# Attention scores in two 64-row tiles of the array, with the exponential banks and the maximum banks paired, and another slot order

## The reference, cut to what matters

```
def mha(x, mask, Wi, bi, Wo, bo):          # encoder: 16 heads of 8 features, causal, ALiBi bias
    q, k, v = split(x @ Wi.T + bi)
    scores = q @ k.T / sqrt(8) + mask      # per head, 256 x 256
    return (softmax(scores) @ v) @ Wo.T + bo
for i in range(4):
    x = x + mha(layer_norm(x), ...)
    x = x + gelu(layer_norm(x) @ ffn1.T + b1) @ ffn2.T + b2      # 128 -> 512 -> 128
return layer_norm(x)
# expert block: 8 heads of 16 features, no mask, q/k/v from a prefix of the features that
# depends on the quarter of the sequence; output projection with the same prefixes
```

## Time and profile before

| | |
|---|---|
| median of three executions | 1793.04 us (1792.7 to 1794.8) |
| profiled execution, its own time | 1786.88 us |
| its span on the core | 1785.0 us |
| instructions | 41176 |
| TensorE busy | 1600.5 us, 90% |
| VectorE / ScalarE / GpSimd busy | 1132.6 / 944.5 / 517.3 us |
| share of DMA queues | 22.8% and 3.3% of 16 engines |

### The profile page before, as it was taken

The page is one execution under the profiler, slowest core; times in us unless marked ns, Lnnn a source line. Parts: engine busy times, 40 slices in busy tenths (PEclk is TensorE's granted clock), DMA queues, the critical chain, the costliest instruction groups (busy, mean ns, idle before and its releaser), DMA issues. The chain is left out here.

```text
span 1785.0 us, 41176 instructions
## 1 busy us (share of the span) xinstructions
PE 1600.5 (90%) x13024; PEld 1146.0 (64%) x13024; DVE 1132.6 (63%) x3106; ACT 944.5 (53%) x1652; POOL 517.3 (29%) x908
## 2 busy tenths in 40 slices
PE   0777776689999999999999999999998999999996
PEld 0444453467777767677777676777776767767774
DVE  6676674466666666666666666666666667666662
ACT  3233332146666646566666565666654656655653
POOL 4222221122222222222222222222222224344433
PEclk9999998799999999999999999999999999999998
DMA  4333331222222222222222222222222222222220
GB/s 115 104 97 105 95 100 42 89 86 76 72 71 72 77 71 71 88 71 71 72 73 78 69 71 87 71 71 72 74 72 74 71 88 78 76 79 77 77 60 13
DMA packets 109892, 137.22 MB, mean 77 GB/s; under 512 B 14272, under 2 KB 95808, under 8 KB 109824
## 3 DMA queue, kind: packets, MB, share of 16 engines
q1 hardware_dynamic: 102176, 115.81, 22.8%
q0 software_dynamic: 7680, 20.98, 3.3%
HBM read 70.54 MB, written 65.01 MB: 76 GB/s over the span
## 5 line engine op out<-in xcount | busy, mean ns | idle before, releaser
L761 ACT ACTIVATE probs<-exp_ps 128x512 f32<-128x512 f32 x896 | 516.0, 596 | 640.8 <-PE exp_ps L872 492.9
L628 DVE TENSOR_REDUCE negm<-mxp 128x2 f32<-128x512 f32 (+1 forms) x1152 | 615.3, 569 | 236.6 <-PE mxp L847 212.3
L841 PE MATMUL mxp<-kst_l,qbd_l 127*128 127x256 f32 x2048 | 454.6, 332 | 33.2 <-DMA qbd_l<-split_L 32.2
L841 PEld LDWEIGHTS mxp<-kst_l,qbd_l 127*128 127x128 f32 x2048 | 334.8, 199 | 56.0 <-DMA qbd_l<-split_L 49.1
L867 PE MATMUL exp_ps<-qbd_l,kst_l 128*128 128x512 f32 x768 | 363.2, 493 | 5.3 <-DMA qbd_l<-negt 4.4
L454 POOL TENSOR_SCALAR veps<-mv 128x2 f32<-128x2 f32 x144 | 31.6, 219 | 958.3 <-DVE mv L586 955.1
L847 PE MATMUL mxp<-maskb,identb 128*128 128x256 bf16 x1024 | 293.7, 287 | 0.0
L872 PE MATMUL exp_ps<-masktb,identb 128*128 128x256 bf16 (+1 forms) x768 | 246.4, 321 | 0.0
L896 PE MATMUL pvp<-probs,vst_l 128*32 128x256 f32 (+1 forms) x4096 | 219.3, 332 | 0.0
L674 DVE COPY ost<-pvp 128x512 f32<-128x512 f32 x80 | 55.3, 692 | 206.3 <-PE pvp L896 206.3
L867 PEld LDWEIGHTS exp_ps<-qbd_l,kst_l 128*128 128x128 f32 x768 | 150.5, 196 | 33.6 <-issue 25.2
(11 more groups left out here) (93 smaller groups left out, 1937.8 us busy)
## 6 DMA issues: line engine op xcount, KB each, us to landing
split_L<-hi SPq DMA_DIRECT2D x256, 128.0 KB, 2.1
kst_l<-split_L SPq DMA_DIRECT2D x64, 384.0 KB
qbd_l<-split_L SPq DMA_DIRECT2D x256, 96.0 KB
split_L<-lo POOLq DMA_DIRECT2D x128, 128.0 KB, 2.1
split_F<-hi SPq DMA_DIRECT2D x64, 128.0 KB, 2.1
kst_f<-split_F SPq DMA_DIRECT2D x16, 384.0 KB, 3.8
qbd_f<-split_F SPq DMA_DIRECT2D x32, 192.0 KB, 4.4
split_F<-lo POOLq DMA_DIRECT2D x32, 128.0 KB, 2.4
```

The source lines that it names most:

```text
L628: dve.tensor_reduce(negm[:, s, qt, h0:h0 + 2], mxp[:, (plan.max_chunks * g + ch) % 3, :].rearrange("p (h t) -> p h t", h=2)[:, :, 0:keys], ...
L761: act.activation(probs[:, g[0], ch, :], exp_ps[:, (plan.exp_chunks * g[0] + ch) % 2, :], ACT.Exp, scale=plan.scale).then_inc(q.b_exp, 1)
L841: last = pe.matmul(mxp[:, bank, k * T:(k + 1) * T], qbd[plan.name][0:MAX_ROW, s, h, qt * P:(qt + 1) * P], kst[plan.name][0:MAX_ROW, s, g[0 ...
```

## The change

Each group of four heads becomes two pairs. One pair lies on partitions 0 to 63 and the other on 64 to 127 (`STRIP`), each with 48 data rows and its own rows for bias and maximum, and every score matmul runs in a tile of 64 rows and 128 columns. There are now four stacks instead of two: for the maxima a dense `qst` and a block-diagonal `kbd`, for the exponentials a dense `kst` and a block-diagonal `qbd`. The block-diagonal operand streams, so that one matmul makes two heads of 256 columns. Both plans make as many maximum banks as exponential banks: 12 in the encoder, 8 in the expert block. An encoder bank is one matmul of 512 columns or two of 256, and its mask is 256 columns, or 512 in the banks 4 and 5 of each half. VectorE reduces 512 values in each.

The exponential bank k of a unit is placed right ahead of the maximum bank k+2 of the next unit, in the other row tile; the mask matmuls of both, on all 128 rows, come after. `pv` has two steps of 32 instructions. `ot` writes into `pvp` (so `pv` waits for `c_attn`). `f1` is cut into two halves, both in `dense[0]`: the first at the end of a slot, the second in the next slot after `v` and `xt`. `hid` and `xn` are single buffers. In the new order `qk+` stands ahead of `op`, and `ln` is one slot earlier (two in the expert block). SyncE issues 12 stack DMAs a unit instead of 5, in two steps, and two for the maxima. Initialisation has other memsets and copies. The main parts:

```
     def slot_steps(self, s, last_layer):
-        ff = self.feed_forward
-        maxes = [("max", s + 1, g, ch) for g in range(GROUPS) for ch in range(self.max_chunks)]
...
+        def scores(exps, maxes):
+            parts = [("exp", s, *divmod(k, self.half_banks)) for k in exps]
+            parts += [("max", s + 1, *divmod(k, self.half_banks)) for k in maxes]
+            masks = [(f"{name}_mask", u, half, bank) for name, u, half, bank in parts] if self.causal else []
+            return parts + masks
+        if self.causal:
+            end, end2, store = (at(k, s - 2) if last_layer else [] for k in ("end", "end+", "store"))
+            return (
+                scores([], [0, 1]) + at("v v+", s + 1) + at("xt", s + 2) + at("wc", s - 1) + [("f1", s - 2, 1)]
+                + at("xt+", s + 2) + [("f1+", s - 2, 1)] + at("ot ot+", s - 1) + scores([0], [2]) + at("qk qk+", s + 2)
+                + at("f2 f2+", s - 2) + at("at at+", s - 1) + scores([1], [3]) + at("op op+", s - 1) + at("stack_exp+", s + 1)
+                + scores([2], [4]) + scores([3], [5]) + end + scores([4], [6]) + at("xn2", s - 1) + scores([5], [7])
+                + scores([6], [8]) + [("pv", s, 0)] + at("ln", s + 3) + scores([7], [9]) + at("xt2 xt2+", s - 1)
+                + scores([8], [10]) + at("xn", s + 3) + end2 + scores([9], [11]) + scores([10], [])
+                + at("stack_max+", s + 2) + at("negt negt+", s + 1) + scores([11], [])
+                + [("f1", s - 1, 0), ("f1+", s - 1, 0), ("pv", s, 1)] + at("pv+", s) + store)
+        return (
+            scores([], [0, 1]) + at("v v+", s + 1) + at("xt xt+", s + 3) + at("stack_exp+", s + 1) + at("stack_max+", s + 2)
+            + at("ot ot+", s - 1)
+            + scores([0], [2]) + at("qk qk+", s + 3) + at("at at+", s - 1) + scores([1], [3]) + at("op op+", s - 1)
+            + scores([2], [4]) + scores([3], [5]) + at("ln", s + 4) + scores([4], [6]) + [("pv", s, 0)]
+            + scores([5], [7]) + at("xn", s + 4) + scores([6], []) + at("negt negt+", s + 1) + scores([7], [])
+            + [("pv", s, 1)] + at("pv+", s))
...
+            def stack(plan, stacked, blocks, parts_of, sc, s, done):
+                rows, members = COPIES * plan.dh, plan.members
+                for strip in range(2):
+                    first = STRIP * strip
+                    sp.dma_start(stacked[plan.name][first:first + DATA_ROWS, s, :, :].bitcast(F32), ...)
+                    for m in range(members):
+                        sp.dma_start(blocks[plan.name][first + rows * m:first + rows * (m + 1), s, :, m, :].bitcast(F32), ...)
...
-            dve.memset(qbd["L"][0:ALIBI_ROW, :, :, :].bitcast(F32), 0.0).then_inc(s_initv, 1)
+            for blocks in (qbd["L"], kbd["L"]):
+                dve.memset(blocks[:].bitcast(F32), 0.0).then_inc(s_zero_l, 1)
+            for stacked in (kst["F"], qst["L"]):
+                for rows_ in constant_rows_of:
+                    dve.memset(stacked[rows_].bitcast(F32), 1.0).then_inc(s_ones, 1)
...
                     elif step == "max":
+                        half, bank = g
+                        k, strip = plan.half_banks * half + bank, (bank + 1) % 2
+                        rows, groups = slice(STRIP * strip, STRIP * strip + plan.max_rows), range(2 * half, 2 * half + 2)
...
+                        for n_job, (gr, qt, keys) in enumerate(jobs):
+                            last = pe.matmul(mxp[:, k % MAX_BANKS, n_job * width:(n_job + 1) * width],
+                                             qst[plan.name][rows, s, gr, qt * P:(qt + 1) * P],
+                                             kbd[plan.name][rows, s, gr, :, keys], start=(n_job == 0), stop=True,
+                                             skip_group_check=True, tile_position=(STRIP * strip, 0))
...
                     elif step == "f1":
                         pe.wait_ge(q.c_xn2t, u + 1)
+                        part, = g
+                        dense_job(0, q.c_gelu, NF, off, 2 * part + 1)
+                        for f in range(2 * part, 2 * part + 2):
```

More of the change, by code:

```diff
@@ L82, in slot_steps @@
[L82 to L92, removed]
@@ L838, in steps @@
-                        qt, pair = ch % NT, ch // NT
-                        for k in range(2):
-                            h = plan.hg * g[0] + 2 * pair + k
-                            last = pe.matmul(mxp[:, bank, k * T:(k + 1) * T],
-                                             qbd[plan.name][0:MAX_ROW, s, h, qt * P:(qt + 1) * P],
-                                             kst[plan.name][0:MAX_ROW, s, g[0], :],
-                                             start=(k == 0), stop=True, skip_group_check=True)
@@ new lines, in steps @@
+                        if k == 0:
+                            pe.wait_ge(q.stk_max[s], 16 * plan.stack_dmas * (r + 1))
+                        before = k - MAX_BANKS if k >= MAX_BANKS else max(range(k, plan.banks, MAX_BANKS)) - plan.banks
+                        wait_past(pe, q.b_red, plan.banks * u + before + 1)
+                        if not plan.causal:
+                            jobs = [(groups[bank // 2], qt, slice(0, T)) for qt in range(NT)]
+                        elif bank < 4:
+                            jobs = [(groups[bank // 2], 1, slice(0, T))]
+                        else:
+                            jobs = [(gr, 0, slice(0, P)) for gr in groups]
@@ new lines, in steps @@
+                        if not plan.causal:
+                            last.then_inc(q.b_max, 1)
+                    elif step == "max_mask":
+                        half, bank = g
+                        k = plan.half_banks * half + bank
+                        o = mxp[:, k % MAX_BANKS, :].rearrange("p (h t) -> p h t", t=T if bank < 4 else P)
+                        heads = o.shape[1]
+                        pe.matmul(o[:, :, P:T] if bank < 4 else o, identb[:, :], maskb[:, 0:heads, :], start=False, stop=True,
+                                  skip_group_check=True).then_inc(q.b_max, 1)
@@ new lines, in steps @@
+                        if not plan.causal:
+                            last.then_inc(q.b_s, 1)
+                    elif step == "exp_mask":
+                        half, bank = g
+                        k = plan.half_banks * half + bank
+                        o = exp_ps[:, k % 2, :].rearrange("p (h t) -> p h t", t=T if bank < 4 else P)
+                        heads = o.shape[1]
+                        pe.matmul(o[:, :, 0:P], identb[:, :], masktb[:, 0:heads, :], start=False, stop=True,
+                                  skip_group_check=True).then_inc(q.b_s, 1)
@@ L901, in steps @@
                         pe.wait_ge(q.c_ost, u + 1)
-                        transposes(mxp[:, OT_BANK, :], [ost[:, s, r, t * P:(t + 1) * P] for t in range(NT) for r in range(2)], q.c_ot)
+                        transposes(pvp[:, :], [ost[:, s, r, t * P:(t + 1) * P] for t in range(NT) for r in range(2)], q.c_ot)
                     elif step == "at":
```

390 lines of the change are left out of this document (198 added, 192 removed).

## The result

The changed kernel takes 2183.53 us (median of 4 runs, 2177.15 to 2188.31) against 1792.87 (1789.09 to 1794.8) before. The ratio is 1.2189, 95% interval [1.2157, 1.222]: 22% slower. The direction was forecast; the size was not, 1980 with a range up to 2085.

The account below looks back on a forecast made before the run. TensorE was taken to bound the encoder before, and waits behind late xb the new slot. Encoder 163, expert 6, start 9 and last layer 16 made 194 over 1786.88: forecast 1980 us, own range 1900 to 2050, whole range 1775 to 2085.

Parts of the forecast that it names:

- The walk: Encoder slot traced as five in-order queues from one second pv's end to the next: 24.5 us, taken as 24.3.
- my encoder terms (163 + 16): Encoder: 63 slots at 2.6 us more make 163; the last layer's final normalisation on VectorE adds 16 us.
- `xb` at 11.9: GpSimd in the encoder slot: xb, behind lo and two DMA issues, ends at 11.9 us; VectorE's addition waits 2.6.
- End of VectorE's stretch at 20.9: Encoder slot: VectorE's addition, statistics, eight maxima and normalisations run from 11.9 to 20.9 us.
- Two changes of tiling for each block at 0.17: TensorE's score blocks: masks on 128 rows force two tiling changes a block; 20 more changes cost 3.4 us a slot.
- Expert slot 15.6: Expert block: slot of 15.6 us, 13.8 if xb weren't late; 15 x 0.4 = 6 us more.
- The start, 9 us: Initialisation: 7 us more for VectorE's memsets and fills, 2 for the longer fill of the pipeline.
- The last layer, 16 us more: Encoder's last layer: VectorE's final normalisation, some 1.5 us a slot, 0.5 already paid, adds 16 us.
- The first: Rival: the slot follows TensorE's work, 18.2 us at 0.05 a tiling change, 21.6 at 0.17; 1660 to 1785 us; chance 0.20.
- The second: Rival: xb isn't late on GpSimd, slot 21.4 to 22.3 us, run around 1830; chance 0.16.
- The third: Rival: row tiles don't run side by side or blocks show weight loads, 2.3 us a slot, 2085 us; chance 0.12.
- the fourth: Rival: the change does nothing, tiling gain and price cancel and waits are hidden, 1789 to 1797 us; chance 0.03.

Follow-up runs that it names:

- filler: Changed kernel plus eight matmuls with overwritten result, placed in the encoder's order where TensorE would wait for the maxima; 2047.0 us, ratio 1.1436.
- masks in row tiles: Kernel with xb and values moved ahead, plus paired blocks' masks added in each bank's own 64-row tile by two matmuls; 1826.94 us, ratio 1.0221.
- `xb` ahead: Changed kernel with GpSimd's xb as its own step ahead of qk, in both parts of the network; 1913.28 us, ratio 1.0686.
- the run with one tile: Kernel with new slot end and full-height masks, but each maximum bank in the same row tile as its paired exponential; 2205.38 us, ratio 1.2274.
- the values ahead: Changed kernel with xb moved ahead, plus the step placing the values (v, v+) ahead of maxima 0 and 1; 1845.92 us, ratio 1.0321.
- the new end: Kernel with row-tile masks, xb and values ahead, plus last blocks ahead of f1's first half and exponentials' stacking at the front; 1929.53 us, ratio 1.0774.
- the releases: Kernel with new slot end and row-tile masks, plus xt and wc ahead of the exponentials' stacking; 1752.81 us (ratio 0.9792), with full masks 1794.62 us.
- the fastest version: Changed kernel with xb and values ahead, masks in row tiles, new slot end and releases ahead of the stacking; 1752.81 us, ratio 0.9792.

## Why the prediction was right in its direction and wrong in its size

**The step that failed** is "I take 24.3 as the steady slot, 2.6 more than 21.72". The walk to it priced every instruction behind the stall at the full clock of the earlier trace rows. The walk itself holds: the filler's slot, in which only the gap is filled, is 24.41 us. What it left out is that TensorE, once it had stood 2.06 us for a free bank, was granted half its clock for the next 6.5 us. That makes the slot 27.3 and the term 5.6 instead of 2.6. Over the encoder the filler's run has 1605.6 us between first and last copy, the changed kernel 1738.1: 132.5 of the 160 us by which my encoder terms (163 + 16) fell short of 339.5. The other 28 lie mainly at the changes of layer and in the first slot: with the filler the distances beyond 63 steady ones are 68 us, before they are 30, and the sum had only the 16 of the last layer for that. I had even named the stall in front of it ("TensorE runs on for three more blocks and then stands for a free `mxp` bank") and had seen an expert slot at 0.90, whose waits are of the same kind, without asking what the stall would do to the clock.

**Point by point.**

- `f1` waits 1.2 us for the values: 0.80 measured.
- `hi` at 7.9: it ended 7.8 after the start of the slot. `xb` at 11.9: 11.9. VectorE's wait 2.6: 2.88, and such waits 57 times in the run.
- End of VectorE's stretch at 20.9: with the filler, 21.0; without it 23.9.
- Two changes of tiling for each block at 0.17: between 0.29 and 0.34 of the block's 0.87 us, so 0.15 to 0.17 each. The rule of the Trainium skill that a change of mode drains the engine ("TensorEngine Tiling (Array Packing)", Key Properties) is in line with that; the page has no size for it, and 0.29 to 0.34 us around 512 + 768 columns is what this trace gives. The up to 2x in the table of the same page of the Trainium skill (Theoretical Speedup) is what the two score streams alone do: 0.01 us apart with opposite tiles, 0.34 with one.
- The masks in row tiles took some of that price off the blocks, but little off the slot: 0.5 us, and 42 us a run with the shorter changes of layer. Blocks are 0.61 to 0.96 us apart, 0.77 on average between 709.14 and 712.21. Two things bound them, and which one does was not taken apart: a maximum takes VectorE 0.68, and a mask of 512 columns is now 1024 columns in one tile, with the scores 1536 columns or 0.64 us.
- TensorE's share near 80% in a steady slot: 23.83 of 27.33, 87%, because half the clock makes busy time too.
- Expert slot 15.6: 17.2, with a clock of 0.80 in the window above. With `xb` ahead it is 15.3 where I had 13.8, so that walk was 1.5 short as well. The stall accounts for about 2 of the 17.2; how much of it is clock wasn't measured.
- The start, 9 us: 16.2. The memsets came as computed (two of 3.47 and four of 1.76 are 14.0), but with the 0.5 to 0.8 us between them the first statistics begin at 18.42 instead of 9.32, and TensorE's first matmul is 9.3 us later, not 7. The other 7 lie between it and the first copy, in the longer fill of the pipeline, for which I had 2.
- The last layer, 16 us more: wrong. Its distances average 25.9 us against 27.3 in a steady slot. With the filler, where the steady slots are at full clock, most are 25.0 to 25.1 against 24.4: its extra work costs some 0.6 us a slot there, and in the changed kernel it doesn't show.
- The passage between the two networks (4.4) and the tail (2.3) weren't in the sum.

**The rivals.** The first, that the slot follows TensorE's work, was worked out as 21.6 at 0.17 a change. With no late wait in the order the same blocks give 21.0 to 21.1 (1794.62 us, no change against before), which by the rival's own terms would be 0.15 a change: near its price, but the kernel as changed isn't in that case. Nor is the price shown by the slot, which is still 20.5 us when most of the changes are gone. The second, `xb` not late, said around 1830; made true, it gave 1913, with the waits for the values and for transfers and a clock of 0.96 that I hadn't priced. The third is excluded by the starts 0.01 us apart and by the run with one tile, the fourth by the result.

**Where the 391 us went,** by what gave them back in turn: 270 with `xb` ahead, 67 with the values ahead, 19 with masks in row tiles, 74 with the new end and the releases. These add up to 430, which passes the kernel before by 35 (1787.75 us beside that run). The shares hold for this order of steps; taken away last instead of given first, `xb` is worth 272.

**Open.** At a change of layer the two longer slots are 28.6 and 25.4 us in the fastest version, 13 us above two steady ones, and 23.4 and 28.3 before, 8 above; there TensorE waits 6.5 and 3.2 us once for SyncE's releases. What they would be with an earlier load wasn't tried. Nor was the start.

## What to carry to other kernels

When a slot is packed to 99% and a change makes the busiest engine wait for some 2 us at once, count the wait twice: once as time, once as what the clock takes from the work behind it. Here waits of 2.06, 2.3 and 3.8 us had that sequel, and one of 0.8 had not. The cure is in the in-order queues: for each instruction that another engine waits for, list what stands ahead of it, DMA issues and bare semaphore increments included; 2.9 us of waiting behind GpSimd's queue cost 270 us, one increment behind six DMA issues 177. And price work that saves columns by its changes of tiling: keep what stands next to each other in one tiling, which was worth 42 us here.

## What the runs showed of the hardware that was not expected

- TensorE busy for 92% of the time (11.17 of 12.18 us) at full clock, then idle for 2.06 us, then 6.53 us at half clock, in nearly every slot of the encoder, for 1.7 ms. An idle stretch of 0.80 at `f1` of the same slot had no such sequel. Useless matmuls in the gap kept the clock at 1.00 and made the run 6% shorter.
- Score matmuls of 53 and 50 rows in opposite row tiles start 0.01 us apart, and the mask follows after 0.44 us as it does behind one bank alone; in one tile they start 0.34 apart, of which 0.21 is the first one's columns.
- From the start of a block of two 512-column banks with their masks to the next: 1.09 us in one tile, 0.87 in opposite tiles with masks of 128 rows, 0.61 at the least with masks in row tiles too.
